# Running the feed-forward part of an image one period behind its search, with the gate taken straight from PSUM, in a conv and token-routed feed-forward kernel

## The reference, cut to what matters

```python
x = x + relu(batchnorm(conv3x3(sign(layernorm_over_channels(x)), sign_weights)))   # statistics over all images
t = tokens(x)                                   # (32, 3136, 128)
n = layernorm(t)                                # per token, over the 128 channels
w = n @ wr + br                                 # one router weight per token
idx = top_k(w, 1568) without its last entry     # 1567 tokens of 3136, per image
y = (gelu(n[idx] @ w1 + b1) @ w2 + b2) * w[idx] # 128 -> 512 -> 128
t = t + n + scatter(y, idx)                     # a token that isn't chosen gets t + n
```

## Time and profile before

| | |
|---|---|
| time, median of 3 executions | 2134.3 us (2131.57 to 2134.45) |
| the profiled execution, its own time | 2142.42 us |
| its span, first to last instruction | 2140.6 us |
| mean granted TensorE clock | 0.986 of full speed |
| busy, share of the span | PE 93%, DVE 78%, ACT 57%, POOL 44% |
| phase 1 | up to about 519.5 us from the span's start |
| `take_router` of image 0, of image 31 | 577.2 us, 2093.1 us |

### The profile page before, as it was taken

How to read it: one execution, slowest core, us unless ns; L and a number is a source line. 1 busy time by engine, 2 the same in 40 slices (tenths; PEclk the granted TensorE clock), 3 DMA queues, 4 the chain that set the end, 5 groups by cost and what they waited for, 6 DMA issues and landing times.

```text
span 2140.6 us, 35882 instructions
## 1 busy us (share of the span) xinstructions
PE 1998.0 (93%) x9515; PEld 1015.2 (47%) x9515; DVE 1671.8 (78%) x4759; ACT 1211.8 (57%) x2030; POOL 934.4 (44%) x714
## 2 busy tenths in 40 slices
PE   6999999996799999999999999999999999999995
PEld 3555555553344444544444444444444444444442
DVE  6777777775688888888888888888887888888875
ACT  3444444443466565666665666666666656666652
POOL 1000000002456555666565565556655656555543
PEclk9999999998899999999999999999999999999998
DMA  4343444443123333333333333332333333333213
GB/s 162 136 180 140 175 153 162 164 151 135 51 87 122 115 120 130 117 112 139 111 120 125 110 127 123 118 128 110 119 132 111 119 125 128 110 123 119 103 69 123
DMA packets 68726, 267.91 MB, mean 125 GB/s; under 512 B 22352, under 2 KB 27184, under 8 KB 64688
## 3 DMA queue, kind: packets, MB, share of 16 engines
q1 hardware_dynamic: 55264, 214.90, 27.5%
q10 hardware_dynamic: 13392, 52.29, 6.6%
HBM read 188.08 MB, written 77.87 MB: 124 GB/s over the span
## 4 chain that ended last, share of the span: by engine, by line
PE 47%; DMA 10%; SPq 6%; DVE 5%; issue 4%; POOL 1%; ACT 1%; ACTq 0%; POOLq 0%; DVEq 0%
PE ps L955 23%; PE ps L944 6%; DMA y<-y_int 5%; PE ps L946 5%; PE ps L945 5%; PE ps L900 5%; SPq L371 4%; DMA w_row<-wrow 3%; DMA wse<-w_row 3%; PE ps L933 2%; SPq L377 1%; DVE base L720 1%; ACT hs L500 1%; DVE rms L697 1%; DVE rms L694 1%
## 5 line engine op out<-in xcount | busy, mean ns | idle before, releaser
L955 PE MATMUL ps<-hs,w_c 128*128 128x448 f32 x1792 | 765.7, 554 | 0.6 <-ACT yo L510 0.6
L500 ACT ACTIVATE hs<-ps,b1c,undo 128x448 f32<-128x448 f32 x896 | 609.8, 719 | 127.4 <-PE ps L946 120.5
L871 PE MATMUL ps<-yo,cwT 128*128 128x448 bf16 x2016 | 425.3, 356 | 0.0
L955 PEld LDWEIGHTS ps<-hs,w_c 128*128 128x128 f32 x1792 | 314.0, 191 | 209.5 <-issue 176.0
L412 POOL TENSOR_TENSOR xb<-xb,zr 128x448 f32<-128x448 f32 x224 | 261.3, 1168 | 271.8 <-ACT zr L528 270.4
L417 POOL TENSOR_TENSOR tl<-tr,th 128x448 f16<-128x448 f32 x224 | 243.5, 1088 | 308.6 <-PE ps L946 192.7
L944 PE MATMUL ps<-th,w_h 128*128 128x448 f16 x896 | 318.4, 355 | 19.5 <-ACT hs L500 19.5
L946 PE MATMUL ps<-th,w_l 128*128 128x448 f16 x896 | 316.3, 353 | 0.0
L945 PE MATMUL ps<-tl,w_h 128*128 128x448 f16 x896 | 316.3, 353 | 0.0
L424 POOL TENSOR_TENSOR yo<-yo,base 128x448 f32<-128x448 f32 x224 | 279.7, 1255 | 77.1 <-DVE yo L797 77.1
L510 ACT ACTIVATE yo<-ps,cols 128x448 f32<-128x448 f32 x224 | 141.8, 633 | 237.9 <-PE ps L955 237.5
(11 more groups left out here) (125 smaller groups left out, 2355.1 us busy)
## 6 DMA issues: line engine op xcount, KB each, us to landing
xb<-x SPq DMA_DIRECT2D x31, 1568.0 KB, 7.5
xb<-x SPq DMA_DIRECT2D x33, 896.0 KB, 4.7
gate_all<-gate_row ACTq DMA_DIRECT2D x32, 896.0 KB, 4.4
result<-yo SPq DMA_DIRECT2D x32, 896.0 KB, 3.5
y_int<-y SPq DMA_DIRECT2D x32, 784.0 KB, 3.7
xb<-x SPq DMA_DIRECT2D x33, 672.0 KB, 4.4
gate_all<-gate_row ACTq DMA_DIRECT2D x32, 672.0 KB, 5.6
result<-yo SPq DMA_DIRECT2D x32, 672.0 KB, 3.0
```

The lines of the kernel that those rows point to most:

```text
L500: nc.scalar.activation(hs[(b + slot) % 2][:, j, :], ps[:, H_BANK + j, 0:T], ACT.Gelu_apprx_tanh, bias=b1c[:, j:j + 1], scale=undo[:, 1:2]) ...
L871: last = M(bank, cwT[:, t, :], sg[b][:, c * ROWS + dy:c * ROWS + dy + ROWS, dx:dx + SIDE], start=t == 0, stop=t == TAPS - 1)
L955: last = M(bank, w2_c[:, j, :], hs[(b + c) % 2][:, j, :], start=first, stop=final)
```

## The change

The period of the feed-forward part is shifted against the rest. `ffn_slot` says which image and slot a step belongs to: with `LAG` = 8, image m's `hidden` and `output` run from step 8 of period m+1 to step 15 of period m+2. The router and the search stay in period m (router one step earlier). There is one more period at the end. When an output chunk leaves PE, the gate of its image is already there, so DVE adds the bias and multiplies with the gate in one instruction from PSUM to `yo`; ACT's copy and the semaphore `y_taken` go, and PE waits for `gated` before it overwrites the bank. `OUT_AT` follows the output steps (23, 31, ... 71). `th` and `tl` exist twice. The second part of the gate's broadcast is a DMA of its own at step 21, and the second half of an image is stored in the next period, ahead of the statistics rows on SP. Several table entries move by one to two steps.

```diff
-RELU_AT = [9, 10, 21, 29, 34, 42, 50]
+RELU_AT = [9, 10, 21, 29, 34, 44, 50]
-STAT_AT = 23
-NORM_AT = [31, 39, 51, 54, 63, 72, 74]
-BASE_AT = [35, 42, 54, 58, 65, 74, 83]
-ROUTER_AT = [26]
-COUNT_AT = [36, 39, 43, 46, 50, 53, 56, 61]
-MASK_AT = 67
+STAT_AT = 22
+NORM_AT = [31, 39, 51, 54, 63, 73, 75]
+BASE_AT = [37, 44, 55, 59, 69, 77, 84]
+ROUTER_AT = [25]
+COUNT_AT = [36, 39, 43, 46, 50, 52, 56, 61]
+MASK_AT = 65
 SCAN_AT = 68
-OUT_AT = [25, 28, 31, 34, 38, 44, 49]
-GATE_OUT_AT = 17
-ROWS_AT = 24
+OUT_AT = [24, 32, 38, 47, 55, 63, 71]
+GATE_OUT_AT = [17, 21]
+LAG = 8
+ROWS_AT = 22
...
-        th = sb("th", [C, TOK], f16)
-        tl = sb("tl", [C, TOK], f16)
+        th = [sb(f"th{b}", [C, TOK], f16) for b in range(2)]
+        tl = [sb(f"tl{b}", [C, TOK], f16) for b in range(2)]
...
+        def ffn_slot(n, b, pos):
+
+            if pos >= LAG:
+                return (n - 1, 1 - b) + divmod(pos - LAG, 2 * NB)
+            return (n - 2, b) + divmod(pos - LAG + POS, 2 * NB)
+
...
-        P2 = (3, n_img - 3)
+        P2 = (4, n_img - 2)
...
                                  mk[:, 5, :]).then_inc(gate_saved, 16)
+                if has(n - 2):
+                    store(n - 2, b, 1)
                 if has(n + 1):
                     sp.wait_ge(rms_ready, n + 2)
...
                     store(n - 1, 1 - b, 0)
-                    store(n - 1, 1 - b, 1)
-
-            pairs(sp, phase2, *P2, -2, n_img + 1)
+
+            pairs(sp, phase2, *P2, -2, n_img + 2)
...
                     for m, mb, c in due(LOW_PART_AT, 1, n, b, pos):
-                        if has(m - 1):
-                            pool.wait_ge(h_done, ((m - 1) * NCH + c + 1) * NB)
-                            pool.wait_ge(w_done, m)
+                        if has(m - 2):
+                            pool.wait_ge(h_done, ((m - 2) * NCH + c + 1) * NB)
                         low_part(m, mb, c)
...
-                    slot, j = divmod(pos, 2 * NB)
-
-                    if j < NB and has(n):
-                        g = n * NCH + slot
+                    m, mb, slot, j = ffn_slot(n, b, pos)
+
+                    if j < NB and has(m):
+                        g = m * NCH + slot
                         act.wait_ge(h_done, g * NB + j + 1)
...
-                    if j == 2 * NB - 1 and (has(n) and slot > 0 or slot == 0 and has(n - 1)):
-
-                        c = (slot - 1) % NCH
-                        m, mb = (n, b) if slot > 0 else (n - 1, 1 - b)
-                        act.wait_ge(y_done, m * NCH + c + 1)
-                        if c == 0 and has(m - 2):
-                            act.wait_ge(out_saved[mb], (m - mb) * 16)
-                        nc.scalar.activation(cut(yo[mb], c), ps[:, Y_BANK, 0:T], ACT.Identity,
-                                             bias=b2_c).then_inc(y_taken, 1)
...
-                    for m, mb, _ in due(GATE_OUT_AT, -1, n, b, pos):
+                    for m, mb, part in due(GATE_OUT_AT, -1, n, b, pos):
                         act.wait_ge(gate_saved, (m + 1) * 16)
                         if has(m - 1):
-                            act.wait_ge(gated, m * NCH)
-                        for part in range(2):
-                            act.dma_start(gate_all[:, PART[part]], g_dram[bass.ds(m, 1), PART[part]]
-                                          .to_broadcast([C, (HALF, NCH - HALF)[part] * T])).then_inc(gate_in[part], 16)
+                            act.wait_ge(gated, (m - 1) * NCH + (HALF, NCH)[part])
+                        act.dma_start(gate_all[:, PART[part]], g_dram[bass.ds(m, 1), PART[part]]
+                                      .to_broadcast([C, (HALF, NCH - HALF)[part] * T])).then_inc(gate_in[part], 16)
...
                 dve.wait_ge(gate_in[c // HALF], (m + 1) * 16)
-                dve.wait_ge(y_taken, g + 1)
-                V.tensor_tensor(cut(yo[b], c), cut(yo[b], c), cut(gate_all, c), ALU.mult).then_inc(gated, 1)
+                dve.wait_ge(y_done, g + 1)
+                if c == 0 and has(m - 2):
+                    dve.wait_ge(out_saved[b], (m - b) * 16)
+                V.scalar_tensor_tensor(cut(yo[b], c), ps[:, Y_BANK, 0:T], b2_c, cut(gate_all, c), ALU.add,
+                                       ALU.mult).then_inc(gated, 1)
...
                 if j == 0:
-                    wait_count(pe, y_taken, g)
+                    wait_count(pe, gated, g)
...
-                    if j < NB and has(n):
-                        hidden(n, b, c, j)
-                    if j >= NB and c > 0 and has(n):
-                        output(n, b, c - 1, j - NB)
-                    if j >= NB and c == 0 and has(n - 1):
-                        output(n - 1, 1 - b, NCH - 1, j - NB)
+                    m, mb, c, j = ffn_slot(n, b, pos)
+                    if j < NB and has(m):
+                        hidden(m, mb, c, j)
+                    if j >= NB and c > 0 and has(m):
+                        output(m, mb, c - 1, j - NB)
+                    if j >= NB and c == 0 and has(m - 1):
+                        output(m - 1, 1 - mb, NCH - 1, j - NB)
...
-            pairs(pe, phase2, *P2, -1, n_img + 1)
+            pairs(pe, phase2, *P2, -1, n_img + 2)
```

More of the change, by code:

```diff
@@ L256, in block_kernel @@
         y_done = sem("y_done")
-        y_taken = sem("y_taken")
         gated = sem("gated")
@@ L416, in low_part @@
                 pool.wait_ge(th_ready, n * NCH + c + 1)
-                nc.gpsimd.tensor_tensor(cut(tl, c), tr[(b + c) % 2][:, :], cut(th, c),
+                nc.gpsimd.tensor_tensor(cut(tl[b], c), tr[(b + c) % 2][:, :], cut(th[b], c),
                                         ALU.subtract).then_inc(tl_ready, 1)
@@ L441, in phase2 @@
                         add_base(m, mb, c)
-            pairs(pool, phase2, *P2, -2, n_img + 1)
+            pairs(pool, phase2, *P2, -2, n_img + 2)
         @block.scalar
@@ L498, in phase2 @@
                             wait_count(act, y_done, g - 1)
-                        nc.scalar.activation(hs[(b + slot) % 2][:, j, :], ps[:, H_BANK + j, 0:T],
+                        nc.scalar.activation(hs[(mb + slot) % 2][:, j, :], ps[:, H_BANK + j, 0:T],
                                              ACT.Gelu_apprx_tanh, bias=b1c[:, j:j + 1],
                                              scale=undo[:, 1:2]).then_inc(h_ready, 1)
-                    if j == 2 * NB - 1 and (has(n) and slot > 0 or slot == 0 and has(n - 1)):
-                        c = (slot - 1) % NCH
-                        m, mb = (n, b) if slot > 0 else (n - 1, 1 - b)
-                        act.wait_ge(y_done, m * NCH + c + 1)
-                        if c == 0 and has(m - 2):
-                            act.wait_ge(out_saved[mb], (m - mb) * 16)
-                        nc.scalar.activation(cut(yo[mb], c), ps[:, Y_BANK, 0:T], ACT.Identity,
-                                             bias=b2_c).then_inc(y_taken, 1)
                     for m, mb, _ in due(ROWS_AT, 1, n, b, pos):
@@ L530, in phase2 @@
                     for m, mb, c in due(LOW_PART_AT, 1, n, b, pos):
-                        if has(m - 1):
-                            act.wait_ge(h_done, ((m - 1) * NCH + c + 1) * NB)
-                            act.wait_ge(w_done, m)
+                        if has(m - 2):
+                            act.wait_ge(h_done, ((m - 2) * NCH + c + 1) * NB)
                         act.wait_ge(t_ready, m * NCH + c + 1)
-                        nc.scalar.activation(cut(th, c), tr[(mb + c) % 2][:, :], ACT.Copy).then_inc(th_ready, 1)
-            pairs(act, phase2, *P2, -2, n_img + 1)
+                        nc.scalar.activation(cut(th[mb], c), tr[(mb + c) % 2][:, :], ACT.Copy).then_inc(th_ready, 1)
+            pairs(act, phase2, *P2, -2, n_img + 2)
         @block.vector
@@ L838, in phase2 @@
                             find_ties(m)
-            for n in range(-1, n_img + 1):
+            for n in range(-1, n_img + 2):
                 phase2(n, n % 2)
@@ L910, in router @@
                     for q, c in enumerate(chunks):
-                        last = M(ps[q * COLS:(q + 1) * COLS, T_BANK, 0:T], w[:, COLS - part:2 * COLS - part], cut(t, c),
+                        last = M(ps[q * COLS:(q + 1) * COLS, T_BANK, 0:T], w[:, COLS - part:2 * COLS - part], cut(t[b], c),
                                  start=part == 0 and i == 0, stop=c + NQ >= NCH and i == 2)
@@ L943, in hidden @@
                 blk = slice(j * C, (j + 1) * C)
-                M(bank, w1_h[:, blk], cut(th, c), start=True, stop=False)
-                M(bank, w1_h[:, blk], cut(tl, c), start=False, stop=False)
-                M(bank, w1_l[:, blk], cut(th, c), start=False, stop=True).then_inc(h_done, 1)
+                M(bank, w1_h[:, blk], cut(th[b], c), start=True, stop=False)
+                M(bank, w1_h[:, blk], cut(tl[b], c), start=False, stop=False)
+                M(bank, w1_l[:, blk], cut(th[b], c), start=False, stop=True).then_inc(h_done, 1)
             def output(n, b, c, j):
@@ L981, in phase2 @@
                 for pos in range(POS):
```

(9 more changed lines are left out.)

## The result

The changed kernel takes 2232.35 us (median of 4, 2218.93 to 2234.73) against 2134.38 us beside it: a ratio of 1.0438, 95% interval [1.0411, 1.0464]. The forecast of 2141 us, within 2114 to 2161, was wrong: slower was right, the size was not.

A forecast was written before the change was run, and what follows sets the result against it. PE was taken to bound the 48.9 us period, with about 2 us idle to gain. Periods -13 us, end +24.5 and fill -5 summed to +6.5, 2141 us from the median, within 2114 to 2161.

The forecast's parts named there:

- The chain and its start: Waits from statistics rows through search and y load to PE: starting one step earlier saves 0.65 us a period.
- the first part: Search and statistics one output step (0.75 us) earlier: PE's two waits shrink by 0 to 0.75 us, taken as 0.65.
- The part on queues: SP's moved store and POOL's low parts behind its add: store wait hidden by 1.8 us, router's second half by 0.4.
- signs under "wrong": First-count wait of 1.3 us or more, PE idle before output or router, w_row over 2.5, period under 48.0.
- under "right": Signs of a correct forecast, among them router results 48.3 to 48.6 us apart and the end about 72 us.
- The term's upper end: Steady term per period, forecast as -0.45 us, with ends -1.05 and +0.6.
- the gate at step 38: DVE waits for chunk 2's output with search work queued behind its gate: 0 to 0.62 us a period, taken as 0.15.
- the round at 52: Search round 5 on DVE moves from step 53 to 52: 0 to 0.75 us a period, taken as 0.15.
- The moved DMAs: Rival: second gate part and store delay rows and router row by 0.8 us, period +0.35, 2164 us; chance 0.11.
- The gate from PSUM: DVE's gate takes 0.62 us instead of median 890 ns, saving DVE 1.9 us a period, worth 0.1 to the period.
- The end: Behind the last router result: a full image of feed-forward still to come, 72.0 us in all, +24.5 (20 to 29).
- The fill: Start without period 0's feed-forward: router 4 us sooner, search 3 us saved, lower clock +2; taken -5 us.

The follow-up runs named there:

- e12: The changed kernel with mean times power on POOL, POOL's residual and last add held until the split, and SP's two stores swapped against e9: 2156.81 us, ratio 1.0064.
- e11: The kernel before, without the lag, with mean times power on POOL, statistics, router and rows one step earlier, POOL's residual held until the split: 2113.15 us, ratio 0.9885.
- e9: The changed kernel with mean times power on POOL, POOL's residual and last add held by a wait for the split, second-half store last on SP: 2194.44 us, ratio 1.0268.
- e7: The changed kernel with POOL's last add and the residual of chunk 2 moved to steps behind the split, second-half store last on SP: 2191.53 us, ratio 1.0218.
- e3: The kernel before with one more POOL add that reads SBUF, needed by nothing, behind the power: 2169.14 us, ratio 1.0127.
- e1: The changed kernel with the product of mean and power moved from DVE to POOL: 2184.5 us, ratio 1.0188.

## Why the prediction was wrong

**The chain and its start: right.** Statistics, router and search a step earlier were to take 0.65 us from the count wait; it fell by 1.1 in the changed kernel. Part of that is the clock: in the five of ten periods without a stretch at half clock the first count still waits 0.5 us, in the others, where PE's work takes longer, 0.1 to 0.2. e12 and e11 have the gain in the period.

**The step that failed** is in the first part: "DVE now waits 1.38 us a period for L920, so its side is ready earlier by more than the step." Two things were wrong in it. The 1.38 contains L920's own 0.36; the slack, from the end of L688 to the start of L920, was 0.79 in the period of the earlier trace rows and about 1.02 in most others. That alone would have done, since the step is 0.75. But DVE's side was taken as it stood, though the same change moved POOL's `add_base` behind the power, where L688 follows. The part on queues costs this move, but only for those that wait for POOL by a semaphore (SP's store, the router's low parts). The SBUF port had no term: what POOL's move does to L688 was put at nothing, without a reason. A row with the price was at hand: L688 took 3.08 us beside POOL in the fill, and the prediction used it there and nowhere else; L683 then took 3.09 in all ten periods looked at. This term alone is 29 x 2.0, and most stretches at half clock follow its gaps. No rival named it, and none of the signs under "wrong" was PE idle before the transposes. None of those signs showed at all: what showed was that the period, 51.42, was not the 48.3 to 48.6 under "right". The term's upper end, +0.6 a period, was also less than its own parts add up to (0.62 + 0.75 = 1.37), and the measured +2.37 lies outside of either.

**The small terms.** The forecast +0.15 for the gate at step 38 and +0.15 for the round at 52 were not separated. The moved DMAs did not hit the search: from the second `w_row` issue to `wse` it is 1.88 us in both kernels. But e9 shows that collision at another load, with a store behind y, for up to 1.6 us a period with what the clock adds.

**The gate from PSUM** takes 679 ns and not 620, with no spread (666 to 684), as this line of after says:

```profile
L794 DVE SCALAR_TENSOR_TENSOR yo<-ps,cols,gate_all x68: 666/679/684, 1104.5 to 1595.8; 128x448 f32<-128x448 f32 x68
```

I had let the row of another operation decide (a product of two tensors, without the bias). The same operation with both inputs in SBUF, `base`, takes 615 in the median, so PSUM costs it 0.064 us. The estimate from the Trainium skill (VectorE: DVE Perf Modes, section on the TRN2 errata) was 0.065 and was right here. It changes no sum: PE waits for no gate in the middle of the changed kernel.

**The end** was 74.8 for 72.0. Step by step it held: the chunks at the end are 5.28 us apart, and behind PE's last output come 5.4 us, for 5.5. What was short is PE's own work, 67.7 us busy for the 65.3 of `hidden` and `output` that I had listed: the last image's search also stands in it (2.6 us of matmuls), and I had given that 1.2 us of waits. **The fill** gave 2.9 to the first router result for 4, and 0.15 in the next interval for 3: that interval did not get shorter with PE's feed-forward away (48.89 for 49.04); in e12, with the lock gone, it was 47.82. What sets it was not separated. The first feed-forward did begin at the lower clock: 0.50 was granted from 603.3, where it starts, to 607.3 us and from 614.2 to 617.6, by estimate (half of that time) at most 3.7 us for the +2.

**Taken together:** e12 against before is -2.5 (fill), -1.2 (first interval), -16.8 (29 x -0.58), +26.4 (end) and -0.4 (last interval), +5.5 us by the spans, where the forecast had -5, -13 and +24.5, +6.5. That the sums meet this closely is in part luck, since e12 also has a cure that the forecast didn't know: e11, the same cure without the lag, is 29.5 us under the kernel before by the spans. Beside e11 the lag costs e12 0.27 us a period, where the forecast's terms for it add up to +0.2 (-0.1 + 0.15 + 0.15), and 26.9 us at the end. So the terms that the model had were of the right size, and the miss, 85.7 us or some thirteen times the forecast's answer, is mostly the one resource that it left out.

## What to carry to other kernels

When an instruction is moved on one engine, ask not only who waits for its result but what stands beside it at its new place: here POOL's reads of SBUF and DVE's instructions with two SBUF inputs, or casts. A tiny DVE instruction on the chain can last as long as POOL's whole run of readers; keep such a run away from it by a wait for the chain's own semaphore, and look where the released work (a store, an add) then lands. And a duration that is strange in one place of the trace, as 3.08 for 1.01 here, is a price: look for every place at which the change can bring it about.

## What was not expected of the hardware

How long a blocked DVE instruction is held varies. Behind the power of the changed kernel it stood through three POOL readers back to back (3.09 us), in e7 through two (2.00). But in e3, with readers as close behind one another, L690 got its turn behind the first in five of ten periods (0.96) and behind the second in the other five (1.90), and the split's last instruction in e1 behind one (1.11). What decides between these was not found. And 2 us of idle time of PE can cost more than 2 us: the granted clock fell to 0.50 for 3.4 us within 1.1 us of ten of the 30 gaps of 1.9 us or more in the middle periods of the changed kernel; in e7, with no gap of that length there, it never fell.
